# Folding the edges of 28 blocks through a matrix of counts, and storing rows as three bf16 pieces

## What is computed

```python
def _sage_layer(x, src, dst, inv_deg, W_self, W_neigh, b):
    agg = jax.ops.segment_sum(x[src], dst, num_segments=N_NODES)
    mean = agg * inv_deg[:, None]
    return x @ W_self + mean @ W_neigh + b
h = relu(_sage_layer(features, ...)); h = relu(_sage_layer(h, ...)); h = _sage_layer(h, ...)
```

## Time and profile before

| | us |
|---|---|
| median of 3 runs (4306.01 to 4308.9) | 4306.53 |
| profiled execution, its own time | 4308.08 |
| its span, first to last instruction | 4306.3 |
| first gather from `h_table`, layer 0 | 68.66 |
| first one-hot product of layer 1 | 1047.05 |
| first one-hot product of layer 2 | 2025.96 |
| last gather of layer 2 | 2981.12 |
| first gather of the attention part | 2995.02 |

### The profile page before, as it was taken

The page is one execution under the profiler, slowest core; times in us unless marked ns, Lnnn a source line. Parts: engine busy times, 40 slices in busy tenths (PEclk is TensorE's granted clock), DMA queues, the critical chain, the costliest instruction groups (busy, mean ns, idle before and its releaser), DMA issues. The chain is left out here.

```text
span 4306.3 us, 75198 instructions
## 1 busy us (share of the span) xinstructions
PE 3277.9 (76%) x13728; PEld 2372.7 (55%) x13729; DVE 2147.4 (50%) x6078; ACT 487.8 (11%) x1111; POOL 3020.7 (70%) x3154
## 2 busy tenths in 40 slices
PE   3777777777777777777788778887777777776798
PEld 2565555555555555555566555565655555555544
DVE  6434333333333333333455555545577777777733
ACT  4000000000000000000011101101011111111122
POOL 5777777777777777777777777776777777777200
PEclk9888889898888888888999999999888889898999
DMA  6444434435344344344444444445655555554411
GB/s 202 121 136 124 124 106 124 125 105 143 105 125 125 105 125 124 106 125 127 130 140 136 142 136 136 142 135 155 162 147 157 148 159 147 157 146 138 127 60 60
DMA packets 284796, 563.69 MB, mean 131 GB/s; under 512 B 104638, under 2 KB 176133, under 8 KB 279691
## 3 DMA queue, kind: packets, MB, share of 16 engines
q0 software_dynamic: 150528, 414.45, 34.0%
q10 hardware_dynamic: 70180, 89.46, 6.3%
q1 hardware_dynamic: 63974, 58.59, 4.4%
HBM read 487.19 MB, written 73.45 MB: 130 GB/s over the span
## 5 line engine op out<-in xcount | busy, mean ns | idle before, releaser
L763 POOL DMA_INDIRECT arena<-h_table,idx_v x2292 | 2174.3, 949 | 726.3 <-issue 694.0
L895 PE MATMUL banks<-arena 128*128 x5856 | 1544.9, 420 | 617.9 <-SPq L790 506.0
L895 PEld LDWEIGHTS banks<-arena 128*128 128x128 f32 x5856 | 1171.5, 208 | 957.2 <-issue 774.4
L842 DVE TENSOR_SCALAR arena<-iota_t,dst_e 128x128 f32<-128x128 f32 x2928 | 846.8, 310 | 821.7 <-PE banks L895 575.9
L1278 POOL DMA_INDIRECT arena<-vs_table,idx_v x764 | 765.0, 1001 | 232.8 <-issue 228.8
L1496 PE MATMUL banks<-arena 128*128 x1952 | 518.8, 416 | 52.8 <-DVE arena L1840 52.6
L1496 PEld LDWEIGHTS banks<-arena 128*128 128x128 f32 x1952 | 366.5, 199 | 192.5 <-issue 120.4
L916 PE MATMUL banks<-arena,lhs 128*128 128x256 f32 x1176 | 339.6, 439 | 5.0 <-ACT lhs L1016 0.2
L948 DVE TENSOR_SCALAR small<-banks 128x1 f32<-128x1 f32 x147 | 23.2, 158 | 638.7 <-PE banks L897 638.7
L1016 ACT ACTIVATE lhs<-banks 128x512 f32<-128x512 f32 x147 | 87.8, 597 | 2073.7 <-PE banks L907 2073.5
L916 PEld LDWEIGHTS banks<-arena,lhs 128*128 128x128 f32 x1176 | 240.5, 215 | 100.8 <-ACT lhs L1016 64.8
(11 more groups left out here) (263 smaller groups left out, 2468.4 us busy)
## 6 DMA issues: line engine op xcount, KB each, us to landing
arena<-h_table,idx_v POOLq DMA_INDIRECT x2292
arena<-dst_dram SPq DMA_DIRECT2D x14, 1792.0 KB
arena<-vs_table,idx_v POOLq DMA_INDIRECT x764
h_table<-arena ACTq DMA_DIRECT2D x11, 1024.0 KB, 7.4
h_early<-arena ACTq DMA_DIRECT2D x10, 1024.0 KB
vs_table<-arena ACTq DMA_DIRECT2D x49, 132.0 KB
x_dram<-arena ACTq DMA_DIRECT2D x49, 128.0 KB
hln_dram<-arena ACTq DMA_DIRECT2D x49, 128.0 KB
```

What stands on the lines that cost most here:

```text
L763: pool.indirect_dma_start(ring[:, s * BJ + j, 0:width], None, table, bass.IndirectOffsetOnAxis(idx_v[:, half, n * BJ + j:n * BJ + j + 1], ...
L842: dve.tensor_scalar(onehot[:, j, :], iota_t[:], dst_e[:, bass.ds(b * BJ + j, 1)], None, ALU.is_equal).then_inc(W["onehot_made"], 1)
L895: pe.matmul(agg[:, 0:D + 1], onehot[:, j, :], ring[:, (b % SLOTS) * BJ + j, 0:D + 1], start=False, stop=False).then_inc(W["onehot_used"], 1)
```

## The change

For 28 of the 196 blocks (every seventh one, moved to the next where a block spans more than 41 nodes, `COUNT_W = 41`), layers 1 and 2 no longer gather rows. Instead:

- **Tables** (`pick_tables_vector`, 62 chained DVE steps, and `pick_tables_tensor`, 52 small matmuls in six turns) choose the blocks and write the list of the other 168 blocks and of 3 virtual blocks that stand for the 28 x 41 = 1148 destinations of the chosen ones. They run behind tile 4 of layer 0; `batch_tables_vector` moves from behind tile 7 to behind tile 2, `late_ends` from behind tile 15 to behind tile 6.
- **Counts**: behind tiles 8 to 23 of layer 0, a matrix of counts is made, how often each of the 6272 source nodes occurs for each of the 1148 destinations. Per block 4 columns, per column one 128x128 and one 128x2016 one-hot on DVE (int16 in, bf16 out, 2 buffers each) and 4 matmuls of 512 columns (the last 480) into four banks; ACT copies the banks as int16 to a stage of 7 blocks, which one DMA of 6272 runs of 574 B stores.
- **Fold**: 9 float32 matmuls of 256 columns per source tile (`fold_tensor`) multiply the counts with the rows of the layer just made, 49 times for layer 1's input and 49 times for layer 2's. In layer 0 two source tiles are folded behind each of tiles 25 to 47, in layer 1 one behind each tile. ACT loads the counts of a source tile (294 KB) and turns them into float32.
- **Pieces**: layers 1 and 2 read rows of 1536 B, three bf16 pieces whose sum is the float32 row. ACT writes the first with the ReLU, DVE the other two in three steps (`split_vector`); ACT stores each tile on its own, twice. The one-hots of the gathered blocks become bf16, and a pair is 3 bf16 matmuls with the same one-hot. The virtual blocks stay float32. The last tile's share (`late_rows`) goes through all three pieces, 12 rounds in place of 4.
- **Split of tile 47**: it is made behind the first one-hots of tile 48.
- `late_setup_scalar` stays behind tile 7, and `batch_tables_scalar` now follows it at once, with a wait for its stores to have landed (`marks_out`).

The core of the diff:

```diff
+COUNT_W = 41
+TABLES_AT, PICK_AT, LATE_AT, COUNT_FROM = 3, 5, 7, 8
+COUNT_GROUP = 7
...
+    tables = [dram("h_table0", (NP, D))] + [dram(f"h_table{i}", (NP, PW)) for i in range(1, 3)]
+    early_tables = [None] + [dram(f"h_early{i}", (NP, PW)) for i in range(1, 3)]
...
+        def count_block_vector(dve, i):
+            for j in range(BJ):
+                at = bass.ds(i * BJ + j, 1)
+                dve.wait_ge(counted, i * BJ + (COUNTED + j - 1))
+                dve.tensor_scalar(low_hot[j % 2], count_iota[:, 0, 0:P], count_low[:, at], None, ALU.is_equal).then_inc(coded, 1)
+                dve.tensor_scalar(count_hot[j % 2].rearrange("p (c w) -> p c w", w=GAP), count_iota, count_code[:, at], None, ALU.is_equal).then_inc(coded, 1)
+        def count_block_tensor(pe, i):
+            pe.wait_ge(counts_taken, i + TAKEN)
...
+                for n in range(0, HOT_W, BE):
+                    to = min(n + BE, HOT_W)
+                    last = pe.matmul(banks[:, 4 + n // BE, 0:to - n], low_hot[j % 2], count_hot[j % 2][:, n:to], start=j == 0, stop=j == BJ - 1)
+                last.then_inc(counted, 1)
...
+            if c == 0:
...
+            act.activation(count_stage[:, :, c * COUNT_W:(c + 1) * COUNT_W],
+                           banks[:, 4:8, :].rearrange("p b n -> p (b n)")[:, 0:NT * COUNT_W].rearrange("p (t w) -> p t w", w=COUNT_W),
+                           ACT.Copy).then_inc(counts_taken, 1)
...
+            act.dma_start(counts_dram[:, :, bass.ds(q * (COUNT_GROUP * COUNT_W), COUNT_GROUP * COUNT_W)].rearrange("t p c -> p t c"),
+                          count_stage).then_inc(counts_out, 16)
...
+            s = m * 2 + half
...
+            if more:
...
+            pe.wait_ge(W["h_made"], since("h_made", l, s + 1))
+            pe.wait_ge(counts_ready, s + (READY + l * NT + 1))
+            apart(pe)
+            for c in range(CSLOTS):
+                n = min(P, CCOLS - c * P)
+                last = pe.matmul(banks[0:n, 3 + c // 2, c % 2 * D:c % 2 * D + D], counts[half][:, c * P:c * P + n], h_nodes[:, s, :],
+                                 start=False, stop=False)
...
+            dve.tensor_copy(virtual[:, 0:CSLOTS, :],
+                            banks[:, 3:8, :].rearrange("p b n -> p (b n)")[:, 0:CSLOTS * D].rearrange("p (c d) -> p c d", d=D)
+                            ).then_inc(rows_folded, 1)
...
+                b, m = r // PARTS, r % PARTS
+                if r > 1:
+                    pe.wait_ge(late_added, 2 * ((l - 1) * LATE * PARTS + r - 1))
                 for j in range(BJ):
-                    last = pe.matmul(banks[:, late_banks(l, b)[j // 2], (j % 2) * D:(j % 2 + 1) * D],
...
                 last.then_inc(late_found, 1)
...
+        def split_vector(dve, l, t):
+            hi, mid, lo = (parts[:, bass.ds(t % 2, 1), m, :].rearrange("p o d -> p (o d)") for m in range(PARTS))
+            dve.wait_ge(W["h_made"], since("h_made", l, t + 1))
+            dve.tensor_tensor(mid, h_nodes[:, t, :], hi, ALU.subtract).then_inc(part_step, 1)
+            dve.tensor_tensor(left_over, h_nodes[:, t, :], hi, ALU.subtract).then_inc(part_step, 1)
+            dve.wait_ge(part_step, PART_STEPS + 2 * (l * NT + t) + 2)
+            dve.tensor_tensor(lo, left_over, mid, ALU.subtract).then_inc(parts_made, 1)
...
+            dve.wait_ge(W["base_moved"], since("base_moved", w, t + 1))
+            apart(dve)
+            with dve.Fori(b0, b1 + 1) as b:
...
+            b0, b1, off = span_of(dve, t, 1)
+            with dve.Fori(b0, b1 + 1) as b:
+                of_block(b, off, hot16)
...
+                pe.matmul(agg[:, 0:D], zeros[:, 0:P], zeros[:, 0:D], start=True, stop=False)
+                for h in range(2):
+                    b0, b1, off = span_of(pe, t, h)
+                    with pe.Fori(b0, b1 + 1) as b:
+                        pe.wait_ge(W["rows_ready"], since("rows_ready", l, b % NB2 + 1))
+                        at = b % SLOTS if h == 1 else within(pe, b - NB2, 0, NV - 1)
+                        for j in range(BJ):
+                            pe.wait_ge(W["onehot_made"], pair_at("onehot_made", l, b, off, j + 1))
+                            if h == 1:
+                                for m in range(PARTS):
+                                    last = pe.matmul(agg[:, 0:D], hot16[:, j, :], ring_parts[:, at * BJ + j, m, :], start=False, stop=False)
+                            else:
+                                last = pe.matmul(agg[:, 0:D], onehot[:, j, :], virtual[:, at * BJ + j, :], start=False, stop=False)
+                            last.then_inc(W["onehot_used"], 1)
+                pe.matmul(agg[:, 0:D], zeros[:, 0:P], zeros[:, 0:D], start=False, stop=True).then_inc(W["agg_done"], 1)
...
+                        for c in group_blocks(r):
+                            count_block_tensor(pe, q * COUNT_GROUP + c)
+                step(FOLD_FROM - 1)
+                pe.wait_ge(counts_taken, TAKEN + NC)
+                fold_open(pe)
+                with pe.Fori(FOLD_FROM, NT - 1) as t:
                     step(t)
+                    fold_tensor(pe, 0, t - FOLD_FROM, 0)
+                    fold_tensor(pe, 0, t - FOLD_FROM, 1)
+                fold_tensor(pe, 0, NT // 2 - 1, 0)
+                step(NT - 1)
+                fold_tensor(pe, 0, NT // 2 - 1, 1)
+                fold_tensor(pe, 0, NT // 2, 0)
+                fold_close(pe)
             elif l == 1:
-                first_and_rest(pe, NT, step)
+                step(0)
...
+                step(1)
+                fold_tensor(pe, 1, 0, 0)
+                with pe.Fori(1, NT // 2) as m:
+                    step(m * 2)
+                    fold_tensor(pe, 1, m - 1, 1)
+                    step(m * 2 + 1)
+                    fold_tensor(pe, 1, m, 0)
+                step(NT - 1)
...
+                        step(q * 4 + (COUNT_FROM + r))
+                        for c in group_blocks(r):
+                            count_block_vector(dve, q * COUNT_GROUP + c)
+                steps(FOLD_FROM - 1, NT - 1)
+                onehots(dve, l, NT - 1, *base_and_span(dve, l, NT - 1), behind_first=lambda: split_vector(dve, l, NT - 2))
+                means(NT - 1)
+                split_vector(dve, l, NT - 1)
...
+            def store_parts(t):
+                act.wait_ge(parts_made, parts_at(l, t + 1))
                 if not isinstance(t, int) or t < NT - 1:
-                    act.dma_start(early[:, bass.ds(t, n), :], h_nodes[:, bass.ds(t, n), :]).then_inc(W["stored"], 16)
-                act.dma_start(to[:, bass.ds(t, n), :], h_nodes[:, bass.ds(t, n), :]).then_inc(last_stored[l], 16)
...
             def step(t):
                 own_rows(t)
+                if there(t - 2):
+                    act.wait_ge(W["stored"], since("stored", l, 16 * (t - 1)))
+                    act.wait_ge(last_stored[l], 16 * (t - 1))
+                if there(t - 1):
+                    store_parts(t - 1)
                 take_turned(t)
...
+                act.activation(parts[:, bass.ds(t % 2, 1), 0, :].rearrange("p o d -> p (o d)"), dense[:, 0:D], ACT.Relu)
                 act.activation(h_nodes[:, t, :], dense[:, 0:D], ACT.Relu).then_inc(W["h_made"], 1)
...
+                late_setup_scalar(act)
+                batch_tables_scalar(act)
+                act.wait_ge(marks_out, 64)
+                with act.Fori(1, 3) as g:
+                    with act.Fori(g * 2 - 2, g * 2) as q:
+                        for r in range(4):
+                            step(q * 4 + (COUNT_FROM + r))
+                            for c in group_blocks(r):
+                                count_block_scalar(act, q, c)
+                        counts_store(act, q)
+                step(FOLD_FROM - 1)
+                act.wait_ge(counts_out, COUNTS_OUT + 16 * COUNT_GROUPS)
+                for half in range(2):
+                    counts_load(act, half, half)
+                with act.Fori(FOLD_FROM, 4 * GS) as t:
```

502 lines of the change are left out of this document (422 added, 80 removed).

## The result

The changed kernel takes **4791.03 us** (median of 4 runs, 4783.19 to 4794.16), the kernel before 4306.27 beside it (4305.71 to 4308.9): 1.112 times the time before, interval 1.110 to 1.114. It is **slower by 485 us**; I had forecast 4226 with a range up to 4310. The profiled execution of the changed kernel took 4791.19 us, its span is 4789.4. Of the experiments, fold_f32, best1 and best2 were timed four times and give an interval; the others are single executions, so a difference of under some 10 us, the spread of the changed kernel's own runs, says nothing there. Four kernels (two_wide, layer0_edits, layer2_edits, best1) ran first on a chip on which the kernel before took 6566 us; their second runs, with _b, had it at 4307 and are the ones read here.

A forecast was written before the change was run, and what follows sets the result against it. POOL's gathers, by number rather than bytes, were taken to bound the three layers. Layer 1 starting 175 us later, less 114 gained in layer 1 and 142 in layer 2, gives -81 us: forecast 4226, range 4135 to 4310.

The forecast's parts named there:

- ACT's 23 us: Layer 0, tile 8: PE waits while ACT issues setup DMAs and table stores behind tile 7; 23 us lost (17 to 28).
- the tiles with counts: Layer 0, tiles 8 to 23: counting lengthens each tile by 9.7 us on average, to 22.8 us, above POOL's 20.0.
- pick_tables: Layer 0, behind tile 4: 62 chained DVE steps and six PE turns stall 35 us (24 to 42).
- the four stores: Layer 0: each group's count store takes 27 us; ACT's next first copy waits for it, 11 us lost, four times.
- The boundary: Between layers: from the last close to the next layer's first product, 36 us in place of 23.1.
- the pair at 0.36: Layer 1 on PE: a pair of three bf16 pieces takes 0.36 us, 6.4 us a tile, giving a tile of 17.0 us.
- PE issue binds in layer 1: Rival: PE's instruction issue sets the pace; at 0.45 us a pair a tile takes 18.6 us, total 4304 at worst; chance 0.15.
- PE's sequencer never shows at 0.436: Layer 1: argument against PE's issue binding, that its sequencer is not seen with float32 pairs of 0.436 us.
- PE needs some 15 us: Layer 2: without a fold PE takes some 15 us a tile against POOL's 17.2, so the layer takes 827 us, 142 gained.
- 0.4 for a second table lookup: Layer 1, PE's time per tile: looking up the second list adds 0.4 us.
- Wide rows and the shared port: Layers 1 and 2: 1536 B gathers cost 5 us, 64 if width slowed them 5%; DVE's new work could slow POOL.
- The rival for "slower": Layers 1 and 2: POOL's gathers wait for DVE holding the shared port; 0.15 us a gather costs 193 us, 4420; chance 0.10.

The follow-up runs named there:

- fold_f32: Changed kernel with the folded product alone: gathered rows stay float32, one float32 matmul a pair, no pieces; 4566.31 us, 1.059 times before.
- best1: fold_f32 with the edits of layer0_edits and layer2_edits added; 4286.97 us, 0.995 of before.
- best2: best1 with the table picking cut into six pieces behind tiles 2 to 7, late_ends behind tile 7, ACT's setup DMAs in five portions; 4275.39 us, 0.992 of before.
- two_wide: Changed kernel with two matmuls a listed pair in place of three, the first of 512 columns; 4646.25 us.
- layer0_edits: Changed kernel with counts laid out in DRAM by groups and ACT's setup DMAs and table stores behind tile 4; 4698.1 us.
- layer2_edits: Changed kernel with one lookup a list in place of two, and layer 2's residual behind the first listed block's one-hots; 4682.02 us.

## Why the prediction was wrong

- **Layer 0 right in kind, 33 us short.** The tables' stall, ACT's 23 us (21), the tiles with counts (24 to 26 us with two blocks for 24.3, 18.0 with one for 18.3, ACT's copy at 1.89), the fold of 4.05 and the tiles 25 to 47 (most 20.9, mean 21.1, against 21.3) came out. Mis-sized: `pick_tables` at 48 us for 35, since PE's turns held DVE for some 22 us where I had put 11 (how much of that is the clock of 0.50 and how much the matmuls themselves, no run separates); the four stores at 65 us for 44, by another mechanism than I had; `late_ends` at 7 for 12, to the good. Tile 48 closed at 1221.8, inside the bound of 1130 to 1230, and was to close at 1186.
- **The boundary right**: 33.6 us from close to first product, forecast 36.
- **Layer 1: the step that failed is the pair at 0.36.** The prediction names the rival, "PE issue binds in layer 1", and stops it at 0.45 us a pair, "0.5 if instructions bind". Within a block the pair is at 0.49; with the turn of the loop, which a float32 pair of 0.436 had hidden, 0.66. The pieces of a tile took 10.9 us in place of 6.4, and the tile 21.0 in place of 17.0. I had taken "PE's sequencer never shows at 0.436" as evidence against. It is none: what hides behind 0.4 us of array time says nothing of its length. The order of the instructions showed 3 addresses, 3 weight loads and 3 matmuls where there had been a third of that, and the bound from above should have been three times the float32 pair, 1.3 us; that rival would have ended well above before. What the count alone would not have told is that the addresses themselves are short and cost by taking away the queue's lead.
- **Layer 2: the step that failed is "PE needs some 15 us", by the same pair and by a wait put at nothing.** The 15 go by a pair at 0.36; by a float32 pair they are 16.3, and best1's tile of 18.9 us less 2.3 of waits for DVE is 16.6, so PE's other work was right. At the 0.62 us a pair of layer 1 the pieces are 4.6 us more than forecast, an estimate, and DVE's serial work, which the change had moved ahead of the listed one-hots, held PE for 1.3 + 3.7 us in the tile shown: together 24.6, measured 24.3. The two overlap: with the fold alone, without pieces, the tile still takes 22.8. The prediction had "0.4 for a second table lookup", in PE's time; a lookup on DVE was 1.9 to 2.5 us in the trace.
- **Wide rows and the shared port** did not come: 961 ns a gather, 1.25 us apart when POOL doesn't wait. The rival for "slower" had the right sign with the wrong mechanism.

Still open: what brought the clock down in layer 0 with the layer 2 edits; what a longer queue time at the turn of the loop consists of (0.87 us with twelve addresses, 0.74 without the waits); and what best1's layers would take with the two edits of layer 2 taken one at a time.

## What to carry over

Before cutting one matmul into several shorter ones, count the instructions of PE's queue for each (address, weight load, matmul, wait) and price them from a stretch where the array does not hide them; where rows exist only with long matmuls, the price is unknown from above and the range must say so. Ask too whether the queue still gets ahead of the array: what it does ahead of time is free, and what it does behind is not. A wait that the profile gives to another engine is tested by looking at when that engine was done. When a second list or phase is put into a tile, walk down the order of the waiting engine and ask what now stands ahead of the operation that the others wait for.

## What the hardware showed

- In a row of bf16 matmuls of 256 columns, each with its weights, one starts 0.109 us after the other; with an address computed for each, 0.124, and then PE's queue has no lead: the sum and wait of a pair add 0.12 us and the turn of the loop 0.75. With one computed address for three matmuls the step stays at 0.109 and the turn adds 0.31.
- Halving the columns of a bound queue made the kernel slower by 161 us: the granted clock fell from 0.99 to 0.72 in layer 1 and to 0.65 in layer 2.
- A DMA of 6272 runs of 574 B is issued in 0.40 us, and the next issue on the same queue then takes 11 to 17 us; behind the same bytes in long runs none takes over 3.
